# A two-layer language-model tower on one NeuronCore: the tables that give every engine its order are solved anew, with the filler products at other places

## The chip, the cores and the metric

One core of a Trainium2 chip runs the whole program. The metric is the device time of one execution in microseconds (us); the time before is the median of three runs. Five engines work side by side, each through its own list of instructions and in that order alone: TensorE (PE in the profile, with its weight loads as PEld), VectorE (DVE), ScalarE (ACT), GpSimd (POOL) and SyncE (SP), which here only starts DMA transfers. They wait for one another by semaphores.

## The reference

16 sequences of 128 tokens with 256 features go through an embedding with layer norm and four residual blocks. Cut to what matters:

```python
h = tok(x, mask, itok)                       # three table rows added, layer norm
h = h + attn0(layernorm(h))                  # linear attention with random features, relu
h = h + ffn0(layernorm(h))                   # the two nearest of 32 prototypes, rank 16 each
h = h + attn1(layernorm(h))                  # causal softmax attention, 16 heads, rotary
h = h + ffn1(layernorm(h))                   # 256-1024-256 with ternary weights
```

Keys of attn0 share one maximum a sequence, and a sequence needs nothing of another, so each sequence is a tile of its own.

## The kernel before, in words

The kernel works on 16 tiles of 128 tokens by 256 features, kept in one SBUF tensor `hres`. A tile passes through some 130 steps with short names; each name is one branch of the `step` function of its engine. Products that need more than half precision are split into a high and a low half (`xTP`, `wqkT_hi`, `wqkT_lo` and so on), three products for one. The steps that the prediction speaks of are, in the order of one tile:

- embedding: `g` (POOL, two gathers), `e2`, `Est`, `Eag`, `Ers`, `Exn`, `esc`, `eh`
- first attention: `Pst`, `Pag`, `Prs`, `Pxn` (normalised tile `xnP`), `Ptr` or `Phi`, `Plo` and the DMA transposition `PT`, then `qk` and `v` (PE products, L1438), `qhi` and `qlo` (halves of query and key, ACT L1258 and DVE L908), `qT` (DMA transposition, L510), `fQ` and `fK` (features, L1450), `qd` and `kd`, `kmxT`, `kmr`, `kbc` (maximum of the keys, L1605, L937, L1619), `ctx`, `o`, `ont`, `of` (L1637 to L1676)
- prototypes: `Fst` to `Fxn` (`xnF`), `Ftr` (L1706), `prt`, `fh`, `hg`, `hgT` (DMA), `y` (L1778)
- second attention: `Rtr`, `rqk`, `rot`, `rT1` and `rT2` (DMA, `rT<-split`), `s1` (L1898), `ngm`, `rT3` (DMA), `s2` (L1921), `pvx`, `pvT`, `wo`
- last block: `Mtr`, `m1` (L2015), `m2` (L2033), `ob`, and the store `st` (L550).

Steps that are done once prepare weights: `zo1`, `zf1`, `zr3` and others on DVE, `yp1`, `yp2`, `yf1` on ACT, `xo1` (L1469), `xo2` (L1477, L1480) and `xt` (L1487) on PE. `xo1` multiplies the two output matrices of the first attention and waits for the second group of loads (the last is `protoT`). `yp1` makes `wqkT_hi` and `zp1` makes `wqkT_lo`, which `qk` needs.

What sets the order is the table `ORDER`: a string of step names for each engine. `due(engine)` reads it from left to right and gives each name the next tile that has not had it. So the steps of different tiles are interleaved (six or seven tiles are in work at a time), and no engine ever takes a step out of its string's order. A waiting step holds all that stand behind it on its engine.

For the first and the last tiles (`BY_PE`) transpositions are made on PE, for the rest by DMA from SP. All DMAs of SP are started in the order of its string; a transposition that waits for its data holds later ones.

Two tables add products of zeros that nothing reads: `warm_up(94)` runs 94 of them (128x512) at the start (L1461), and `WARM[step][tile]` says how many stand ahead of a step (L1500), after the wait for the PSUM bank and before the wait for the step's data. PE's clock, as the profile shows it, has two levels: 1.2 and 2.4 GHz (a granted clock of 0.50 and 1.00).

## Time and profile before

| what | before |
|---|---|
| median of 3 runs | 462.4 us (460.88 to 462.6) |
| profiled execution, its own time | 467.38 us |
| its span, first to last instruction | 465.6 us |
| PE busy | 395.4 us (85%), 5011 products |
| DVE, ACT, POOL busy | 349.0, 275.8, 293.7 us |
| mean granted clock | 0.956 |

The profiled execution is one run, and 4.98 us above the median. Its span is what the rows below lie in. A busy PE includes the filler products, 94 at the start and 53 later. The profile page also shows that the last 100 us keep DVE, ACT and POOL less busy than the middle, since the tiles run out there.

### The profile page before, as it was taken

The page shows a single profiled execution, that of the slowest core. Times are in us where ns is not written, and L with a number is a line of the kernel's source. Part 1 is how long each engine was busy: PE and PEld are TensorE (multiplying, and loading weights), DVE is VectorE, ACT ScalarE, POOL GpSimd, SP SyncE. Part 2 cuts the span into 40 slices and gives each one's busy share as a digit, 9 for nine tenths or more (in the row PEclk, how much of TensorE's full clock was granted, in tenths as well). Part 3 has the DMA queues.
Part 4 walks back from the last instruction along what each step waited for, and adds up shares of the span by engine and source line. Part 5 has one row for each costly group of instructions (what it writes and reads, how often), then busy time and mean ns, then how long its engine had stood idle before and what let it go on. Part 6 is the DMA issues. An engine that isn't in the chain of part 4 may idle for free.

```text
span 465.6 us, 13969 instructions
## 1 busy us (share of the span) xinstructions
PE 395.4 (85%) x5011; PEld 273.8 (59%) x5011; DVE 349.0 (75%) x937; ACT 275.8 (59%) x605; POOL 293.7 (63%) x431
## 2 busy tenths in 40 slices
...
GB/s 137 175 270 163 181 72 57 69 83 92 85 156 63 129 83 105 136 118 139 115 111 111 117 128 95 109 132 125 86 117 94 101 131 104 72 3 46 14 13 35
DMA packets 145844, 48.56 MB, mean 104 GB/s; under 512 B 137264, under 2 KB 143216, under 8 KB 145776
## 3 DMA queue, kind: packets, MB, share of 16 engines
...
## 4 chain that ended last, share of the span: by engine, by line
PE 33%; POOL 18%; DMA 14%; issue 14%; DVE 9%; ACT 6%; SPq 3%; another core or an unknown queue 1%; POOLq 0%; ACTq 0%; DVEq 0%
PE PS L1438 9%; DMA hgT<-hgs 4%; PE PS L2033 4%; PE PS L1778 3%; DMA qkT<-qs 3%; DMA rT<-split 2%; POOL split L693 2%; PE PS L2015 2%; PE PS L1506 2%; PE PS L1936 2%; DMA xTP<-xsP 2%; POOL wneg L608 2%; POOL stage_f L690 2%; POOL hgs L676 1%; PE PS L1898 1%
## 5 line engine op out<-in xcount | busy, mean ns | idle before, releaser
L1084 DVE TENSOR_REDUCE split<-PS 128x16 f16<-128x2048 f32 x16 | 36.8, 2298 | 6.9 <-PE PS L1506 6.5
L680 POOL TENSOR_TENSOR rstdR<-rstdR,consts 128x1 f32<-128x1 f32 x16 | 8.8, 553 | 37.9 <-DVE rstdR L1043 37.9
L690 POOL TENSOR_TENSOR stage_f<-stage_f 128x512 f32<-128x512 f32 x16 | 20.4, 1272 | 18.7 <-DVE stage_f L1072 8.8
L2015 PE MATMUL PS<-xTM,w1q 128*128 128x128 f16 x512 | 31.4, 219 | 0.0
L2015 PEld LDWEIGHTS PS<-xTM,w1q 128*128 128x128 f16 x512 | 28.6, 98 | 3.6 <-issue 3.6
L1778 PE MATMUL PS<-faT_hi,hgT 128*128 128x256 f16 x128 | 26.7, 295 | 4.0 <-DMA hgT<-hgs 4.0
L1172 ACT ACTIVATE xnR<-hres,nmeanR,rstdR 128x256 f32<-128x256 f32 x16 | 9.6, 599 | 32.1 <-POOL nmeanR L682 32.1
L1438 PE MATMUL PS<-wqkT_hi,xTP 128*128 128x512 f16 x64 | 22.6, 395 | 4.6 <-DMA xTP<-xsP 3.7
L658 POOL TENSOR_TENSOR qe<-qef,qe 128x704 f16<-128x704 f32 x16 | 24.3, 1521 | 1.8 <-issue 1.0
L1637 PEld LDWEIGHTS PS<-va,kp 128*88 128x88 f32 x256 | 21.8, 158 | 2.6 <-issue 0.7
L1461 PE MATMUL PS<-warm 128*128 128x512 f16 x94 | 22.0, 398 | 1.4 <-DVE warm L1139 1.4
L1438 PE MATMUL PS<-rwqk_hi,xTR 128*128 128x512 f16 x64 | 22.6, 394 | 0.4 <-DVE xTR L1051 0.3
L1169 ACT ACTIVATE split<-stage_f 128x256 f16<-128x256 f32 (+1 forms) x48 | 22.0, 481 | 1.4 <-POOL stage_f L690 1.4
L1637 PE MATMUL PS<-va,kp 128*88 128x34 f32 x256 | 22.3, 242 | 0.4 <-issue 0.4
L693 POOL TENSOR_TENSOR split<-stage_f,split 128x512 f16<-128x512 f32 x16 | 18.9, 1182 | 5.3 <-ACT split L1169 5.1
L669 POOL TENSOR_TENSOR dist<-near,halves 128x2 f32<-128x2 f32 x16 | 11.4, 713 | 16.4 <-ACT near L1314 16.3
L1438 PE MATMUL PS<-fbT_hi,xTF 128*128 128x512 f16 x64 | 21.7, 379 | 0.0
L676 POOL TENSOR_TENSOR hgs<-hg,hgs 128x512 f16<-128x512 f32 x16 | 18.5, 1157 | 4.3 <-ACT hgs L1169 4.1
L1450 PE MATMUL PS<-proj_hi,qkT 64*128 64x88 f16 x256 | 14.8, 208 | 6.2 <-DMA qkT<-qs 3.7
...
L700 POOL TENSOR_TENSOR rstdM<-rstdM,consts 128x1 f32<-128x1 f32 x16 | 8.8, 548 | 16.8 <-DVE rstdM L1110 16.8
L1172 ACT ACTIVATE ehat<-esum,nmeanE,rstdE 128x256 f32<-128x256 f32 x16 | 9.5, 592 | 16.7 <-POOL nmeanE L630 16.7
...
## 6 DMA issues: line engine op xcount, KB each, us to landing
...
rT<-split SPq DMA_TRANSPOSE x26, 2.9
```

The source lines that it names most:

```text
L658: g.tensor_tensor(of_pairs(qel), in_pairs(qef), of_pairs(qeh), ALU.subtract).then_inc(qel_ok, 1)
L676: g.tensor_tensor(hgs[:, R2:2 * R2], hg[:, :], hgs[:, 0:R2], ALU.subtract).then_inc(hgl_ok, 1)
L690: g.tensor_tensor(rot[:, :, :].rearrange("p h d -> p (h d)"), rc[:, :], rs[:, :], ALU.add).then_inc(rot_ok, 1)
L693: g.tensor_tensor(slots(32), rot[:, :, :], slots(16), ALU.subtract).then_inc(rl_ok, 1)
L1084: v.tensor_reduce(slots(SLOT - DH)[:, 0:H, DH - 1].rearrange("p (c j) -> p j c", j=4), PS[:, BANK["s1"]:BANK["s1"] + 4, :].rearrange("p j ...
L1169: return a.activation(dst, src, ACT.Copy)
L1172: a.activation(dst, src, ACT.Identity, bias=nmean[x][:, 0:1], scale=rstd[x][:, 1:2]).then_inc(xn_ok[x], 1)
L1438: last = pe.matmul(dst, xT[x][:, xp, :], wp[:, c, :], start=(n == 0), stop=(n == 3 * KC - 1 and bias is None))
L1461: last = pe.matmul(PS[:, SET_BANK, :], warm[:, 0:P], warm[:, :], start=(j == 0), stop=(j == n - 1))
L1637: last = pe.matmul(PS[0:MP, BANK["ctx"], 2 * VA * j:2 * VA * (j + 1)], kp[:, (j % 2 * 4 + j // 2) * MP:(j % 2 * 4 + j // 2 + 1) * MP], va[ ...
L1778: pe.matmul(PS[:, BANK["y"], 0:D], hgT[:, xp, :], wp[:, c, :], start=(c == 0 and xp == 0 and wp is whi["faT"]), stop=False)
L2015: last = pe.matmul(PS[:, BANK["m1"] + f // 4, f % 4 * P:(f % 4 + 1) * P], w1q[:, n % KC, f * P:(f + 1) * P], xT["M"][:, n, :], start=False ...
```

## The change

Every string of `ORDER` is written anew. The steps are the same ones, each as often as before, and every engine still has all of its steps (398 on PE, 737 on DVE, 566 on ACT, 307 on POOL, 152 on SP). 222 of PE's steps stand at another place, by 0.8 places in the mean; 574 of DVE's, by 2.6. The banks of PSUM and the set of transpositions made on PE are untouched. Of the filler products 98 instead of 94 stand at the start, and 39 instead of 53 later, at other steps.

```diff
 ORDER = {
...
     "SP": """
-        lR qT PT lW1 qT qp lW2 PT qp qT PT qp qT hgT PT rT3 qp qT rT2 rT1 hgT onT rT3 PT qp qT rT2 rT1 hgT onT rT3 PT qp qT rT2 rT1 hgT onT rT3 PT qp
...
+        lR qT PT lW1 qT qp lW2 PT qp qT PT qp qT hgT rT3 PT qp qT rT1 rT2 hgT onT rT3 PT qp qT rT2 rT1 hgT onT rT3 PT qp qT rT2 rT1 hgT onT rT3 PT qp
...
     "PE": """
-        xo1 Ptr qk xo2 v fQ qk fK kmxT v kbc fQ ctx fK o ont of kmxT v kbc qk Ftr xt prt ctx fh o hgTp ont fQ y of fK qk kmxT v Rtr kbc Ftr rqk prt
...
+        Ptr qk v xo1 fQ qk fK xo2 kmxT kbc ctx fQ o ont v fK of kmxT kbc qk Ftr prt ctx fh xt v o hgTp ont fQ y of v fK qk kmxT Rtr kbc Ftr rqk prt
...
 WARM = {
-    "qk": {0: 4},
-    "v": {0: 7},
-    "fQ": {0: 9},
-    "kmxT": {0: 4, 2: 2, 3: 4},
-    "ctx": {0: 5, 2: 1},
-    "ont": {0: 2},
-    "Ftr": {0: 2},
+    "qk": {0: 3},
+    "fQ": {0: 8},
+    "ctx": {0: 8, 1: 2, 2: 2},
+    "ont": {0: 3},
+    "Ftr": {0: 4},
     "prt": {0: 3},
-    "rT2p": {0: 2},
-    "y": {1: 3},
+    "rT2p": {0: 1},
...
-            warm_up(94)
+            warm_up(98)
```

**Place 1, the start.** PE from its first instruction, before. `warm` are the fillers, `xnP` the first tile's normalised rows, `wqkT` rows the first `qk`.

```order
L1461 MATMUL PS<-warm 128x512 x94
L1469 MATMUL PS<-wfcT,stage_p 128x256 x4
L1534 MATMUL PS<-ident,xnP 128x128 x2
L1500 MATMUL PS<-warm 128x512 x4
L1438 MATMUL PS<-wqkT_hi,xTP 128x512
L1438 MATMUL PS<-wqkT_lo,xTP 128x512
L1438 MATMUL PS<-wqkT_hi,xTP 128x512 x2
L1438 MATMUL PS<-wqkT_lo,xTP 128x512
L1438 MATMUL PS<-wqkT_hi,xTP 128x512
L1442 MATMUL PS<-rows_all,pick 128x512
```

And now:

```order
L1458 MATMUL PS<-warm 128x512 x98
L1531 MATMUL PS<-ident,xnP 128x128 x2
L1497 MATMUL PS<-warm 128x512 x3
L1435 MATMUL PS<-wqkT_hi,xTP 128x512
L1435 MATMUL PS<-wqkT_lo,xTP 128x512
L1435 MATMUL PS<-wqkT_hi,xTP 128x512 x2
L1435 MATMUL PS<-wqkT_lo,xTP 128x512
L1435 MATMUL PS<-wqkT_hi,xTP 128x512
L1439 MATMUL PS<-rows_all,pick 128x512
```

`xo1` (`wfcT,stage_p`) stood between the fillers and the transposition of `xnP`; now it stands behind `qk` and `v` of tile 0 (not shown), and `v` no longer waits behind `xo2`.

DVE in the same place, before, from the first instruction of `zo1` to `qlo` of tile 0 (`qs<-PS,qs`); `PV` (`xTP`), `Pst` and `Pag` stand ahead of it:

```order
L799 TENSOR_TENSOR proto_sq<-protoT 128x64
L800 TENSOR_SCALAR protoT<-protoT 128x64
L803 TENSOR_TENSOR wneg<-stage_p,bv 128x512
L805 TENSOR_REDUCE bo_v<-wneg 128x2
L807 TENSOR_TENSOR bo_v<-bo_v,bo 128x2
L876 BN_STATS statsE<-esum 128x6
L793 TENSOR_SCALAR proj_hi<-proj 128x176
L795 SCALAR_TENSOR_TENSOR proj_lo<-proj,proj_hi 128x176
L880 BN_AGGR mvE<-statsE 128x2
L882 TENSOR_SCALAR rstdE<-mvE 128x1
L908 SCALAR_TENSOR_TENSOR qs<-PS,qs 128x32x16
```

And now, from `PV` of tile 0 on:

```order
L901 TENSOR_TENSOR xTP<-PS,xTP 128x256
L887 BN_STATS statsP<-hres 128x6
L891 BN_AGGR mvP<-statsP 128x2
L893 TENSOR_SCALAR rstdP<-mvP 128x1
L905 SCALAR_TENSOR_TENSOR qs<-PS,qs 128x32x16
L873 BN_STATS statsE<-esum 128x6
L834 CAST iota_row<-iota_i 1x32
L877 BN_AGGR mvE<-statsE 128x2
L879 TENSOR_SCALAR rstdE<-mvE 128x1
```

`qlo` stood behind the five instructions of `zo1`, behind `Est`, `zp4` (`proj_hi`, `proj_lo`) and `Eag`; now it follows `Pst` and `Pag` directly, and `zo1` comes after it. On ACT `yf1` (`fbT_hi`) moved in the same way from ahead of `qhi` to behind it, and `yp1` (`wqkT_hi`) to behind the second tile's `Exn`.

**Place 2, PE ahead of the prototypes of tile 0.** From `kmxT` of tile 1 on, before:

```order
L1605 MATMUL PS<-ident,kmx 16x128
L1438 MATMUL PS<-wvT_hi,xTP 128x256
L1438 MATMUL PS<-wvT_lo,xTP 128x256
L1438 MATMUL PS<-wvT_hi,xTP 128x256 x2
L1438 MATMUL PS<-wvT_lo,xTP 128x256
L1438 MATMUL PS<-wvT_hi,xTP 128x256
L1619 MATMUL PS<-ident,kmx_row 128x16
L1438 MATMUL PS<-wqkT_hi,xTP 128x512
```

And now, as far as `Ftr` of tile 0 (`ident,xnF`):

```order
L1602 MATMUL PS<-ident,kmx 16x128
L1616 MATMUL PS<-ident,kmx_row 128x16
L1435 MATMUL PS<-wqkT_hi,xTP 128x512
L1435 MATMUL PS<-wqkT_lo,xTP 128x512
L1435 MATMUL PS<-wqkT_hi,xTP 128x512 x2
L1435 MATMUL PS<-wqkT_lo,xTP 128x512
L1435 MATMUL PS<-wqkT_hi,xTP 128x512
L1439 MATMUL PS<-rows_all,pick 128x512
L1497 MATMUL PS<-warm 128x512 x4
L1703 MATMUL PS<-ident,xnF 128x128 x2
```

`v` of tile 2 (the `wvT` rows) stood between `kmxT` and `kbc` of tile 1 and so ahead of `Ftr` of tile 0, with `qk` of tile 2 and two fillers behind it; now it comes after `fh` of tile 0, four fillers stand ahead of `Ftr`, and `kbc` follows `kmxT` with nothing between. In later tiles too (3 to 6, 12 and 13) a `v` left the place between `kmxT` and `kbc`.

**Place 3, the end.** PE from `m1` of tile 14, before:

```order
L2011 MATMUL PS<-sel,b1h 128x512 x2
L2015 MATMUL PS<-xTM,w1q 128x128 x32
L2033 MATMUL PS<-w2q,stage_r 128x256 x16
L1993 MATMUL PS<-ident,xnM 128x128 x2
L1500 MATMUL PS<-warm 128x512
L2011 MATMUL PS<-sel,b1h 128x512 x2
L2015 MATMUL PS<-xTM,w1q 128x128 x32
L2033 MATMUL PS<-w2q,hidden 128x256 x16
L1500 MATMUL PS<-warm 128x512
L2033 MATMUL PS<-w2q,stage_r 128x256 x16
```

And now:

```order
L2008 MATMUL PS<-sel,b1h 128x512 x2
L2012 MATMUL PS<-xTM,w1q 128x128 x32
L2030 MATMUL PS<-w2q,stage_r 128x256 x16
L1990 MATMUL PS<-ident,xnM 128x128 x2
L2030 MATMUL PS<-w2q,hidden 128x256 x16
L1497 MATMUL PS<-warm 128x512
L2008 MATMUL PS<-sel,b1h 128x512 x2
L2012 MATMUL PS<-xTM,w1q 128x128 x32
L1497 MATMUL PS<-warm 128x512
L2030 MATMUL PS<-w2q,stage_r 128x256 x16
```

`m2` of tile 14 stood behind `m1` of tile 15 and now stands ahead of it, right behind the last transposition (`ident,xnM`).

## Rows read from the trace of the kernel before

**Rows 1.** The page: its first line, and the engines' busy time

```profile
span 465.6 us, 13969 instructions
...
PE 395.4 (85%) x5011; PEld 273.8 (59%) x5011; DVE 349.0 (75%) x937; ACT 275.8 (59%) x605; POOL 293.7 (63%) x431
```

**Rows 2.** Busy time by stage; columns: stretch, length, PE, PEld, DVE, ACT, POOL, granted clock, DMA, GB/s

```profile
28.50:69.00 40.50, 28.75 (x229) 15.95 (x230) 31.65 (x80) 24.83 (x46) 32.29 (x44) 0.83 0.62 160
69.00:108.60 39.60, 31.43 (x353) 19.70 (x352) 34.10 (x86) 22.58 (x54) 34.56 (x33) 0.91 0.40 63
108.60:365.50 256.90, 226.62 (x3182) 163.50 (x3179) 209.53 (x564) 172.61 (x388) 173.03 (x262) 0.97 0.65 112
365.50:465.60 100.10, 83.64 (x1151) 63.13 (x1149) 61.86 (x156) 50.78 (x112) 33.66 (x51) 0.98 0.27 56
```

**Rows 3.** Timeline of PE, start: start, duration, instruction, [idle before <- releaser]

```profile
1.42 21.96 PE L1461 MATMUL PS<-warm 128*128 128x512 f16 x94 [1.42 <-DVE warm L1139]
...
25.25 1.97 PE L1469 MATMUL PS<-wfcT,stage_p 128*128 128x256 f32 x8 [1.86 <-DMA protoT<-in_protoT]
27.05 0.38 PE L1534 MATMUL PS<-ident,xnP 128*128 128x128 f32 x2
...
28.52 0.38 PE L1438 MATMUL PS<-wqkT_hi,xTP 128*128 128x512 f16 x1 [0.23 <-DVE xTP L904]
...
37.19 0.21 PE L1450 MATMUL PS<-proj_hi,qkT 64*128 64x88 f16 x2
```

**Rows 4.** Timelines of ACT and DVE, same stretch

```profile
23.37 0.60 ACT L1172 ACTIVATE xnP<-hres,nmeanP,rstdP 128x256 f32<-128x256 f32 x1 [3.96 <-POOL nmeanP L646]
...
29.75 1.06 ACT L1175 ACTIVATE fbT_hi<-stage_f 128x1024 f16<-128x1024 f32 x1 [1.89 <-DMA stage_f<-in_faT]
30.71 0.58 ACT L1258 ACTIVATE qs<-PS 128x512 f16<-128x512 f32 x1
...
32.51 0.68 DVE L908 SCALAR_TENSOR_TENSOR qs<-PS,qs 128x512 f16<-128x512 f32 x1
...
41.51 0.89 DVE L925 TENSOR_TENSOR qd<-PS,qb 128x704 f32<-128x704 f32 x1
```

**Rows 5.** Timeline of SP, which starts the transfers

```profile
22.51 0.43 SPq L457 DMA_DIRECT2D stage_f<-in_faT  x1
...
33.22 1.57 SPq L510 DMA_TRANSPOSE qkT<-qs  x1
```

**Rows 6.** Timelines of PE and ACT around Ftr of tile 0

```profile
59.88 0.37 PE L1438 MATMUL PS<-wvT_hi,xTP 128*128 128x256 f16 x1 [1.48 <-DMA xTP<-xsP]
...
61.24 0.60 PE L1619 MATMUL PS<-ident,kmx_row 16*128 16x16 f32 x2
...
64.74 1.06 PE L1500 MATMUL PS<-warm 128*128 128x512 f16 x2
65.59 0.55 PE L1706 MATMUL PS<-ident,xnF 128*128 128x128 f32 x2
...
61.89 0.60 ACT L1172 ACTIVATE xnF<-hres,nmeanF,rstdF 128x256 f32<-128x256 f32 x1 [1.05 <-POOL nmeanF L664]
```

**Rows 7.** Busy time by stretch: two spells at a granted clock of 0.50

```profile
52.30:65.90 13.60, 9.96 (x53) 4.88 (x50) 10.24 (x25) 8.00 (x12) 12.54 (x17) 0.50 0.55 140
93.20:100.00 6.80, 6.22 (x67) 4.07 (x68) 5.05 (x10) 3.61 (x8) 6.30 (x8) 0.50 0.62 84
```

**Rows 8.** Waits of PE from 108.6 to 365.5: total, times, longest

```profile
PE PS L1898 <- DMA rT<-split: 6.9, 5, 2.3
PE PS L1778 <- DMA hgT<-hgs: 3.2, 3, 1.7
...
PE PS L1619 <- DVE kmx_row L937: 1.7, 4, 0.6
```

**Rows 9.** Timeline of PE, end

```profile
455.90 0.38 PE L1500 MATMUL PS<-warm 128*128 128x512 f16 x1 [1.09 <-DVE xTM L1118]
...
461.06 1.91 PE L2033 MATMUL PS<-w2q,stage_r 128*128 128x256 f16 x16
```

More of the change, by code:

```diff
@@ L75 @@
+        bb e2 Rrs qel esc Frs bb Ers Prs eh dist rot rl Prs hgl gsl Plo rol onl Mrs e2 Rrs qel Frs Mlo esc dist rot Mrs rl gsl Plo hgl Ers onl rol Mlo
+        eh Rrs Frs qel Mrs bb rot dist esc eh rl hgl gsl rol Prs onl Rrs Plo qel Frs bb Mlo bb rot dist rl Mrs rol hgl gsl onl bb Mlo Prs Rrs Plo qel
+        Frs Mrs rot dist rl gsl hgl rol bb qel Rrs Mlo Frs Mrs rot dist rl hgl gsl rol Rrs Mlo Frs Mrs bb dist rot rl gsl hgl Mlo Rrs rot rl bb Mrs
+        Mrs Mrs bb bb bb
     """,
     "DVE": """
-        zi Est Eag zp3 Pst zp1 Est Pag zm Eag PV Pst Pag zo1 Est zp4 Eag qlo zo2 zp2 zf1 zt Pst Est diag Eag qmx Pag qb qd qlo kmx kmr kb kd Est zf2
@@ L78 @@
-        qmx diag qb qd Eag ctl zo3 od on zr3 zf3 oV Pst kmx Pag hP Fst Fag kmr zr1 Est kb kd Eag zr2 FT Pst nd2 top qlo tix gap gt hg ctl zth od Pag
-        on ws hgTb diag oV qmx qb qd hF hP Rst Fst Rag Fag kmx kmr zq1 kb RT kd qlo FT rs2 rs1 nd2 rc top zq2 tix gap ctl gt ws hg od zq3 on rT2b diag
-        rT1b qmx qb oV qd ngm hF Rst Rag hP kmx Fst Fag kmr Pst RT Est kb kd zrm FT Eag rs1 nd2 top rc rs2 tix Pag gap qlo zq4 gt hg ctl ws qmx diag
-        qb od rd on qd ro ngm rV hF Rst Rag kmx hR hP kmr Est Fst Fag RT Mst kb kd rc rs2 Mag rs1 FT nd2 top qlo tix gap gt hg Pst Eag diag rd ctl Pag
```

103 lines of the change are left out of this document (52 added, 51 removed).

## The prediction

> **What bounds the kernel now.** I read the page first, for who is busiest: PE, 395.4 us of a span of 465.6 [rows 1]. Then busy time by stage, since the share of PE is not one thing [rows 2]. From 108.6 to 365.5, while tiles 4 to 14 follow one another, PE is busy 226.62 of 256.9 us; `qk` of tile 4 starts at 108.6 and that of tile 15 at 365.5, so a tile costs 23.4 us, of which 2.8 are idle. That stage and the last 100 us (83.64 of 100.1 busy) go by PE's work, and the work is the same after the change. From 28.5 to 108.6 it is another matter: PE is busy 60.2 of 80.1 us, with the fillers in it, DVE 65.8 and POOL 66.9. There the first tiles' chains set the pace, from engine to engine, and PE waits. A microsecond saved on the first tile's chain moves all that follows, as long as POOL and DVE, with 13 to 14 idle microseconds each in this stage, can follow.
>
> Third the timelines of the start, for what holds that chain. PE runs its 94 fillers from 1.42 to 23.4, then waits 1.86 for the load of `protoT`, does `xo1` (1.97 us) and only at 27.05 transposes `xnP`, which was there from 23.97 on (23.37 + 0.60); `qk` of tile 0 starts at 28.52 [rows 3, 4]. ACT copies its high half at 30.71, behind `fbT_hi` and a load; DVE makes the low half at 32.51, behind `zo1`; SP starts the transposition `qT` at 33.22, and `fQ` of tile 0 runs at 37.19 [rows 3 to 5].
>
> **The change, part by part.**
>
> 1. *`xo1` behind `qk` and `v`, four more fillers.* The fillers cost 21.96 / 94 = 0.23 us each in that row, so 98 end at 24.3. On ACT the second tile's `Exn` and `yp1` (1.06, as `fbT_hi`, which has its shape) now stand ahead of `xnP`. If they fit into ACT's idle 3.96 us ahead of it, `Ptr` starts at 24.3; if both fall wholly behind, at 23.97 + 0.60 + 1.06 = 25.6. I take 24.5, nearer to the first, since that idle time is longer than both. Gain 27.05 - 24.5 = 2.55 us, between 1.4 and 2.75. What is late next is `zp1`, which waits for `yp1`; `Ptr`'s copies hide most of it.
> 2. *`qlo` ahead of `zo1`, `qhi` ahead of `yf1`.* From the start of `qk` to that of `qlo` it takes 3.99 us now. Without the work ahead it is 1.7 for `qk`, 0.58 for `qhi` and 0.1 of hand-over, 2.4. Gain 1.6. `qT` then starts at 33.22 - 2.55 - 1.6 = 29.1.
> 3. *But `qT` then meets the loads.* At 33.22 nothing is left of them and `fQ` follows 3.97 us after the start of the transfer. At 29.1 the weights of the second attention are still on their way. What a transfer takes in that crowd, the load of `faT` shows: started at 22.51, released ACT at 29.75, 7.2 us. So `fQ` of tile 0 comes between 29.1 + 4.0 = 33.1 and 29.1 + 7.2 = 36.3. A transposition is smaller than that load, but behind it; I take 34.4, a little below the middle. Gain at `fQ`: 37.19 - 34.4 = 2.8, between 0.9 and 4.1.
> 4. *From there to `of` of tile 0.* The same steps in another order. `qd` (41.51) was followed by `kmx` and `kd`; now `Pst`, `qlo` of tile 1, `zr3` and `zo2` come between, and `yo` stands ahead of `ke` on ACT. Against that, `v` of tile 0 and `fQ` no longer stand behind `xo2`, and `zo3` is done ahead of `ctl`. I take the two as equal: nothing, and the 2.8 go on.
> 5. *Ahead of `Ftr` of tile 0.* `xnF` was there at 62.49, `Ftr` ran at 65.59: PE was behind, with `v` of tile 2 (59.88 to 61.24), `kbc`, `qk` and two fillers [rows 6], all at a granted clock of 0.50 [rows 7]. `v` goes, 1.36 us; two more fillers come, 0.43 each at this level and 0.21 at the upper. Gain 0.5 to 0.9; I take 0.7.
> 6. *`kbc` right behind `kmxT`.* Of tiles 3 to 6, 12 and 13 `v` no longer covers `kmr`, so PE waits there about what it waits at the worst now, 0.6 us [rows 8], instead of 0.3: 6 x 0.3 = 1.8 at most. The same `v` now covers other waits of PE (it stands mostly ahead of `kmxT`). Nothing net, the bounds are 0 and 1.8 slower.
> 7. *Fillers.* 10 fewer. They stood where PE waits, so their 2.1 us give nothing back. What they cover if gone is the clock, a rival below.
> 8. *The middle.* All other moves, 574 of DVE's steps among them, shift waits. PE waits there for transfers: 6.9 us in 5 waits for `rT`, 3.2 in 3 for `hgT` [rows 8]. No row tells which end. I take nothing, with one half of these two gone (5.0 faster) and as much again (5.0 slower) as bounds.
> 9. *The end.* `m2` of tile 14 (1.91, as the last one) goes into the idle 1.09 us plus filler ahead of `m1` of tile 15 [rows 9]: `m1` starts 0.5 later and all behind it too. Cost 0.5.
>
> Sum: -2.8 - 0.7 + 0.5 = **-3.0 us**. Against the profiled execution that is 467.38 - 3.0 = 464.4. It stands 4.98 above the median of the runs, 462.4; the same gain from the median gives **459.4 us**.
>
> The Trainium skill speaks against part 3 being free: DMA: Bandwidth & Descriptors, section Issuing engines are not separate DMA queues, says that all transfers run on the same 16 DMA engines and interleave. By that rule the transposition shares with the loads, and the sum would be that of the far end of part 3, with 2.8 - 0.9 = 1.9 us less gained, 461.3.
>
> **Rivals.** *The start's gain is lost on the way* (0.27). The far ends of parts 1 to 3 together, or POOL: it has 66.9 us of work in 80.1, and its long single steps stand in it unmoved, so tiles 1 to 3 may reach 108.6 hardly earlier. For it speaks that tile 1 waits for POOL's chain; against it, 13 us of idle time. Then the time is 461 to 463.
>
> *The middle gets shorter too* (0.16). Half the waits of part 8 go: -3.0 - 5.0 gives 454.4. For it speaks that order is all that these waits depend on; against it, that the rows do not show one that must end.
>
> *The clock* (0.12), slower. Now the lower level of 1.2 GHz holds from 52.3 to 65.9 and from 93.2 to 100.0, in a stage in which PE is idle a quarter of the time [rows 2, 7]. 11 of the fillers that stood ahead of `v` and `kmxT` of tile 0 are gone, and of the 10 of tiles 1 to 3 six. A spell like that at 93.2, with PE busy 6.22 of 6.80 us, holds some 3.1 us that the upper level would have saved. Two more of them in this stage cost 6.2: 459.4 + 6.2 = 465.6. One costs less than the change gains, so two is the point from which it decides. The Trainium skill says of this, in TensorE: Matmul & The Clock Gate, section HAM oscillation, that idle gaps between bursts of products bring the clock down; by that rule fewer fillers in the waiting stage cost time, and the trace agrees in so far as both spells follow waits.
>
> *The middle waits longer* (0.11), slower. Steps that give late transfers room stand further from what they feed; six more waits like those for `rT`, 1.4 us each, and the 0 to 1.8 of part 6 make 459.4 + 8.3 = 467.7; three of them already eat the gain. For it speaks part 6, where products that covered a wait have left it; against it, that PE has 2.8 idle microseconds a tile to take small shifts.
>
> That the change doesn't do what it says is no case of its own: the order of the instructions shows it done.
>
> **How the numbers follow.** The forecast, a gain kept from 2.3 to 5 us, has 0.34. About 0.5% (2.3 us) is what a measurement of this kernel can tell from no change. Faster by more: forecast and shorter middle, 0.34 + 0.16 = 0.50. Within: the lost gain, 0.27. Slower: 0.12 + 0.11 = 0.23. The range takes in the shorter middle nearly whole and the clock's rival, and leaves out the worst of the longer middle: 453.5 to 466.5.
>
> **What would show it.** `Ptr` of tile 0 at 24 to 25.6, `qT` at 29 to 30, `fQ` of tile 0 at 33 to 36.3; `Ftr` of tile 0 at 61 to 63; `qk` of tile 4 at 104 to 106.5; after that still 23.4 us a tile. The clock's rival would show as more than 20.4 us at 0.50 before 108.6. Wrong would be: `qk` of tile 4 at 108 or later (the gain lost), or a tile in the middle that costs less than 23.1 or more than 23.7 us, since ten of them then outweigh the start.

## The result, and the profile after

The changed kernel takes **471.26 us** (470.42 to 472.38, 4 runs) where the kernel before took 462.5 in the same comparison (460.88 to 464.49, 4 runs): a ratio of 1.0154, 95% interval 1.0113 to 1.0195. It is slower; 459.4 us was forecast, in a range that ended at 466.5.

How large the loss is, four runs did not settle. Repeated on three chips beside the kernel before, the same program stood nearer to it. In these tables the medians are over all executions, which spread over some 15 us of either kernel; the ratios and their intervals leave the slower ones out, so for a spread like this I go by the medians.

| the changed kernel | executions | median us | kernel before, same chip | difference | ratio, interval |
|---|---|---|---|---|---|
| first measurement | 4 | 471.26 | 462.5 (4) | +8.8 | 1.0154 [1.0113, 1.0195] |
| `after_again`, chip 4 | 12 | 461.59 | 459.85 (17) | +1.7 | 0.9969 [0.9916, 1.0022] |
| `after_third`, chip 1 | 12 | 466.69 | 464.64 (23) | +2.1 | 0.9993 [0.9941, 1.0044] |
| `after_fourth`, chip 8 | 6 | 469.89 | 464.21 (17) | +5.7 | 1.012 [1.005, 1.019] |

All four differences of the medians point the same way; by the ratios the first and the last measurement are slower and the two between are level with the kernel before. The three repeats, by the means of all executions weighted with their own scatter, give +2.7 us with a 95% margin of 1.5; the first gives +8.7 with 1.7. I take some 3 us, 0.6%, as what the change costs by itself, and come back at the end to what lies above.

**The page of the changed kernel**, against [rows 1]:

```profile
span 470.1 us, 13951 instructions
...
PE 394.0 (84%) x5001; PEld 274.6 (58%) x5001; DVE 348.2 (74%) x937; ACT 274.8 (58%) x605; POOL 293.2 (62%) x431
```

4.5 us more span, with 1.4 us less PE work, and the other engines within 1 us. Nothing was added; the time is in waits.

**Busy time by stage**, cut at the start of `qk` of tile 4 (107.3) and of tile 15 (369.4), against [rows 2]; columns: stretch, length, PE, PEld, DVE, ACT, POOL, granted clock, DMA share, GB/s:

```profile
28.50:69.00 40.50, 27.42 (x227) 16.40 (x225) 30.89 (x79) 25.39 (x51) 30.73 (x43) 0.87 0.64 170
69.00:107.30 38.30, 29.38 (x328) 19.14 (x329) 31.68 (x81) 20.30 (x46) 33.72 (x34) 0.87 0.31 56
107.30:369.40 262.10, 227.07 (x3184) 164.15 (x3185) 210.00 (x567) 173.05 (x393) 173.68 (x264) 0.96 0.63 111
369.40:470.10 100.70, 83.47 (x1151) 62.95 (x1149) 61.99 (x154) 50.15 (x110) 32.90 (x49) 0.98 0.24 53
```

Up to `qk` of tile 4 the change is ahead: 107.3 against 108.6. From there to tile 15 it takes 262.1 us against 256.9, with PE busy 227.07 against 226.62: all but 0.5 of the 5.2 us is idle time of PE, 35.0 us instead of 30.3. The rest is as long as before to within a microsecond.

**The start on PE**, against [rows 3]; columns: start, duration, instruction, [idle before <- releaser]. The line numbers of the changed kernel are lower by 3:

```profile
1.42 23.61 PE L1458 MATMUL PS<-warm 128*128 128x512 f16 x98 [1.42 <-DVE warm L1136]
24.87 0.38 PE L1531 MATMUL PS<-ident,xnP 128*128 128x128 f32 x2
...
26.35 0.38 PE L1435 MATMUL PS<-wqkT_hi,xTP 128*128 128x512 f16 x1 [0.45 <-DVE xTP L901]
...
27.86 0.27 PE L1435 MATMUL PS<-wvT_hi,xTP 128*128 128x256 f16 x1
...
30.24 1.89 PE L1497 MATMUL PS<-warm 128*128 128x512 f16 x8
35.52 0.22 PE L1447 MATMUL PS<-proj_hi,qkT 64*128 64x88 f16 x2 [3.39 <-DMA qkT<-qs]
```

And **ACT, DVE and SP** in the same stretch, against [rows 4, 5]:

```profile
28.06 0.60 ACT L1255 ACTIVATE qs<-PS 128x512 f16<-128x512 f32 x1 [2.38 <-issue]
...
28.69 0.69 DVE L905 SCALAR_TENSOR_TENSOR qs<-PS,qs 128x512 f16<-128x512 f32 x1 [1.75 <-ACT qs L1255]
...
29.40 1.50 SPq L507 DMA_TRANSPOSE qkT<-qs  x1
```

`Ptr` comes 2.2 us earlier, `qlo` 3.8 earlier, SP starts `qT` at 29.40 instead of 33.22. But `fQ` gains only 1.7 us: eight fillers run, and then it still waits 3.39 us for `qkT`, which lands 6.1 us after its start. In the kernel before that transfer landed 3.2 us after its start; `fQ` ran 0.8 us later, right behind nine fillers and not on the landing. The DMA moved 319 GB/s in the 6.1 us from 29.4, and 75 GB/s in the 4.0 us from 33.2 before.

**Ahead of `Ftr` of tile 0** on PE, against [rows 6]:

```profile
60.49 1.03 PE L1497 MATMUL PS<-warm 128*128 128x512 f16 x4
61.35 0.38 PE L1703 MATMUL PS<-ident,xnF 128*128 128x128 f32 x2
```

`Ftr` runs at 61.35, 4.2 us earlier than before.

**Waits of PE in the middle**, 107.3 to 369.4, against [rows 8]; columns: waiting line <- releaser: total us, times, longest:

```profile
PE PS L1918 <- DMA rTm<-split: 6.6, 6, 2.2
PE PS L1895 <- DMA rT<-split: 5.7, 5, 1.7
PE PS L1435 <- DVE hres L1030: 4.4, 4, 1.6
PE PS L1616 <- DVE kmx_row L934: 3.6, 8, 0.5
PE PS L1775 <- DMA hgT<-hgs: 2.5, 2, 2.2
```

The kernel before, from 108.6 to 365.5, in two rows of the same view:

```profile
PE PS L1921 <- DMA rTm<-split: 1.2, 1, 1.2
...
PE PS L1438 <- DVE hres L1033: 0.4, 2, 0.2
```

Two rows are the new ones. L1918 is `s2`, the second pass over the scores of the second attention. It reads `rTm`, which `rT3` transposes once `ngm` has put the negated maxima of `s1` into `split`: 6.6 us, where the same row of the kernel before had 1.2. L1435 <- `hres` L1030 is `wo`, which writes into PSUM bank 7 and so waits until DVE's `hF` has read `y` out of it: 4.4 us, 0.4 before. The row of `kmx_row` doubled, 3.6 in 8 waits for 1.7 in 4; those for `rT` and `hgT` fell by 1.2 and 0.7. The three rows that grew hold 11.3 us more together and PE's idle time only 4.7, so most of what they hold was waited for elsewhere before: a row's growth is not its price.

**The end on PE**, against [rows 9]: the last two `m2` steps. The last one starts 3.4 us later, in a span that is 4.5 us longer.

```profile
458.01 1.92 PE L2030 MATMUL PS<-w2q,hidden 128*128 128x256 f16 x16
...
464.46 1.91 PE L2030 MATMUL PS<-w2q,stage_r 128*128 128x256 f16 x16 [1.89 <-DVE stage_r L1120]
```

### The profile page after: what moved, and what is told of

Same layout as the page of the kernel before. It is cut to its first block, busy times and chain, and to the rows that moved or that the text cites. A ratio compares the mean times of both kernels' runs of the same rounds, so it can differ in the third digit from the quotient of the medians.

```text
span 470.1 us, 13951 instructions
## 1 busy us (share of the span) xinstructions
PE 394.0 (84%) x5001; PEld 274.6 (58%) x5001; DVE 348.2 (74%) x937; ACT 274.8 (58%) x605; POOL 293.2 (62%) x431
## 4 chain that ended last, share of the span: by engine, by line
PE 47%; DVE 16%; DMA 13%; issue 9%; ACT 7%; POOL 4%; SPq 2%; another core or an unknown queue 2%; ACTq 0%; DVEq 0%; POOLq 0%
PE PS L1435 13%; DMA rTm<-split 6%; PE PS L1458 5%; PE PS L2012 4%; DVE split L1081 4%; PE PS L2030 3%; PE PS L1933 3%; PE PS L1634 2%; DMA rT<-split 2%; DMA hgT<-hgs 2%; DMA qkT<-qs 2%; PE PS L1447 2%; PE PS L1918 2%; PE PS L1503 2%
## 5 line engine op out<-in xcount | busy, mean ns | idle before, releaser
L1081 DVE TENSOR_REDUCE split<-PS 128x16 f16<-128x2048 f32 x16 | 36.8, 2297 | 13.7 <-remote 8.2
L1435 PE MATMUL PS<-rwqk_hi,xTR 128*128 128x512 f16 x64 | 25.8, 447 | 0.7 <-DVE xTR L1048 0.3
L1458 PE MATMUL PS<-warm 128*128 128x512 f16 x98 | 23.6, 407 | 1.4 <-DVE warm L1136 1.4
L1435 PE MATMUL PS<-wqkT_hi,xTP 128*128 128x512 f16 x64 | 22.0, 385 | 1.4 <-ACT stage_p L1386 0.8
L1435 PE MATMUL PS<-fbT_hi,xTF 128*128 128x512 f16 x64 | 21.7, 380 | 0.0
L1380 ACT ACTIVATE stage_p<-PS 128x1024 f32<-128x1024 f32 x16 | 16.4, 1023 | 6.6 <-PE PS L1503 6.5
L1447 PEld LDWEIGHTS PS<-proj_hi,qkT 64*128 64x128 f16 x256 | 10.4, 100 | 15.8 <-issue 8.2
```

The lines of the kernel that those rows point to most:

```text
L1081: v.tensor_reduce(slots(SLOT - DH)[:, 0:H, DH - 1].rearrange("p (c j) -> p j c", j=4), PS[:, BANK["s1"]:BANK["s1"] + 4, :].rearrange("p j ...
L1435: last = pe.matmul(dst, xT[x][:, xp, :], wp[:, c, :], start=(n == 0), stop=(n == 3 * KC - 1 and bias is None))
L1447: last = pe.matmul(PS[:, bank + i, MP * c:MP * (c + 1)], qkT[rows_, c0 + c, :], part[rows_, MP * i:MP * (i + 1)], start=(c == 0 and part i ...
L1458: last = pe.matmul(PS[:, SET_BANK, :], warm[:, 0:P], warm[:, :], start=(j == 0), stop=(j == n - 1))
```

## The experiments

Sixteen kernels ran, four to a chip, each with the kernel before beside it. Theory M says that the loss lies in the new order of the middle; theory H that the new head brings it on, whatever comes behind; a third, that the placing of the fillers and with it the clock does. A kernel with two orders in one follows, on every engine, the one up to the instant at which PE starts the named step, and the other behind it; each step still runs once.

| run | chip | executions | median us | before | difference | ratio, interval |
|---|---|---|---|---|---|---|
| `head_new` | 7 | 12 | 458.43 | 459.08 | -0.6 | 0.9978 [0.9938, 1.0018] |
| `head_new2` | 1 | 12 | 464.25 | 464.64 | -0.4 | 0.9953 [0.9908, 0.9997] |
| `head_old` | 7 | 12 | 465.61 | 459.08 | +6.5 | 0.9984 [0.9905, 1.0063] |
| `head_old2` | 8 | 12 | 469.43 | 464.21 | +5.2 | 1.0088 [1.0045, 1.0132] |
| `fill_old` | 7 | 6 | 466.47 | 459.08 | +7.4 | 1.0177 [1.0123, 1.0231] |
| `fill_new` | 1 | 6 | 470.88 | 464.64 | +6.2 | 1.0111 [1.0051, 1.017] |
| `wo_back` | 7 | 12 | 460.87 | 459.08 | +1.8 | 0.9984 [0.987, 1.0099] |
| `wo_back2` | 1 | 6 | 473.24 | 464.64 | +8.6 | 1.0144 [1.0078, 1.021] |
| `wo_ahead` | 4 | 6 | 468.16 | 459.85 | +8.3 | 1.024 [1.0169, 1.0311] |
| `s2_back` | 4 | 7 | 475.14 | 459.85 | +15.3 | 1.0362 [1.0305, 1.0418] |
| `pe_mid_new` | 4 | 6 | 533.75 | 459.85 | +73.9 | 1.1683 [1.1608, 1.1759] |
| `cut8_new` | 8 | 6 | 470.55 | 464.21 | +6.3 | 1.0125 [1.0054, 1.0197] |
| `cut8_old` | 8 | 6 | 473.66 | 464.21 | +9.5 | 1.0233 [1.0159, 1.0306] |

**Head and middle apart.** `head_new` is the changed kernel with the old orders behind `qk` of tile 4. PE's string around the seam:

```diff
-        ctx fh o rT2p rT1p fQ ont s1 of y rv fK s2 Rtr kmxT kbc rqk Ftr qk prt ctx pvx fh pvT o v fQ s1 rv rot_ y of fK wo s2 Rtr kmxT kbc rqk Ftr qk
+        ctx fh o rT2p rT1p fQ ont s1 of y rv fK s2 Rtr kmxT kbc rqk Ftr prt qk fh pvx ctx v pvT fQ o s1 rot_ rv y fK wo of kmxT Rtr s2 kbc rqk Ftr qk
```

> The new orders of all five engines and the new zero products up to qk of tile 4, the old orders behind it. Theory M (the new order of the middle, qk of tile 4 to qk of tile 15, costs the 262.1 us against 256.9 that the two profiles show): the middle falls back to 256 to 258.5 us, qk of tile 4 starts at 106.5 to 108, and the time is that of the kernel before less the 1.3 us of the head, 459.5 to 463. Theory H (what the new head leaves behind, later buffers and other low-clock stretches, slows the tiles after it, whatever their order): the middle stays at 261 to 263 us and the time at 468 to 472.

> The changed head with the old orders from qk of tile 4 on, again. Theory M: 0.1 to 0.5% faster than the kernel before, as the first time (458.4 beside 459.1), and faster than the changed kernel by its whole loss plus the head's gain. If the head's gain does not reach the end: equal to the kernel before within 0.3%.

`head_old` is the mirror image, made in the same way.

> The mirror image: the old orders and zero products up to qk of tile 4, the new orders behind it. Theory M: the middle stays at 261 to 263 us, and the time is 469 to 473. Theory H: the middle is 256 to 258.5 us and the time 461 to 465.

> The old orders and zero products up to qk of tile 4, the new ones behind, a second time. Theory M: slower than the changed kernel by the 1.5 to 4 us of its missing head, and than the kernel before by 1.0 to 1.5%, as the first time (465.6 beside 459.1). If the middle's 259 us against 252 in the profiles so far were chance: within 0.4% of the kernel before.

The middle of `head_new`, from its `qk` of tile 4 to that of tile 15, by busy time and by waits of PE:

```profile
107.80:354.20 246.40, 220.88 (x3183) 160.46 (x3180) 208.55 (x563) 172.20 (x387) 171.92 (x260) 0.99 0.63 115
```

```profile
PE PS L1895 <- DMA rT<-split: 3.6, 5, 1.7
PE PS L1435 <- DMA xTo<-xso: 3.4, 6, 1.0
...
PE PS L1616 <- DVE kmx_row L934: 1.7, 4, 0.6
...
PE PS L1435 <- DVE hres L1030: 0.4, 2, 0.2
```

And `head_old2`, the head and the middle:

```profile
0.00:111.10 111.10, 91.32 (x687) 50.77 (x688) 77.76 (x221) 53.68 (x108) 86.56 (x120) 0.85 0.52 131
111.10:368.80 257.70, 223.11 (x3181) 162.07 (x3178) 209.17 (x564) 171.79 (x389) 173.21 (x262) 0.98 0.61 110
```

And PE's waits in that middle of `head_old2`:

```profile
PE PS L1921 <- DMA rTm<-split: 6.8, 5, 1.9
...
PE PS L1619 <- DVE kmx_row L937: 4.5, 9, 1.0
...
PE PS L1438 <- DVE hres L1033: 3.4, 4, 1.1
```

With the old order the middle is 246.4 us (250.5 the second time), the row of `rTm` is gone from the list and `wo <- hF` is back at 0.4. With the new one behind the old head it is 257.7 (259.7 the first time), the three rows are there, and `head_old` and `head_old2` are 6.5 and 5.2 us slower than the kernel before in their medians, 5.7 us by the means of both (margin 2.0). By its ratio alone, 0.9984 with only two executions in it, `head_old` is not slower; `head_old2` is, 1.0088. That is theory M; H is out, since the new head did not bring the loss with it. A limit stays: a seam may cost something by itself, as those at tile 8 below suggest, and no run prices that for tile 4. `head_new` has a seam too and loses nothing.

Parts of M's forecast failed. `head_old2` should have been 1.5 to 4 us slower than the changed kernel, whose head it lacks, and stands 0.5 us below it on the same chip. Both `head_new` should have kept the head's gain, and are only 0.6 and 0.4 us faster than the kernel before. Their `qk` of tile 4 starts at 107.8 and 111.2, no earlier in the mean than in the kernels with the old head. One thing in it is the cut itself: in the old string, and so in `head_new` too, `prt` stands ahead of that `qk`, in the changed kernel behind it (the diff shows it); with its wait it took 0.6 us in the kernel before and 1.2 in the first `head_new`. Of the kernels that ran, `head_new` is the only one whose median was not above that of the kernel before. By the means of both runs it is 0.9 us faster with a margin of 1.5, a gain that these runs can't tell from zero.

All profiles together, microseconds from `qk` of tile 4 to that of tile 15, each with PE's idle time in it:

| | profiles | length | mean | PE idle, mean | PE busy, mean |
|---|---|---|---|---|---|
| old middle (before, `head_new`, `head_new2`, `fill_new`) | 4 | 256.9, 246.4, 250.5, 255.2 | 252.3 | 28.5 | 223.8 |
| new middle (the changed kernel) | 4 | 262.1, 255.9, 258.4, 261.3 | 259.4 | 33.3 | 226.2 |
| new middle behind the old head | 2 | 259.7, 257.7 | 258.7 | 33.1 | 225.6 |
| new middle, old fillers (`fill_old`) | 1 | 259.2 | 259.2 | 30.9 | 228.3 |

The new middle of the changed kernel costs 7.1 us by the first two rows, 4.8 of it idle time and 2.4 the same products at a lower granted clock. Four profiles a side that scatter so leave a margin of some 7 us, and the two of `head_new` weigh heavily: their middles had 2.8 and 3.4 us at the low level of the clock, the other two old ones 17.1 and 13.7, the seven new ones 10.8 to 24.6. Without `head_new` the difference is 3.3 us. What does not depend on the draw of the profiles is the pattern of waits: `rTm` holds 5.2 to 8.1 us, `kmx_row` 3.6 to 4.5 and `wo <- hF` 1.8 to 4.7 in all seven new middles, and at most 1.2, 1.8 and 0.4 in the four old ones.

The executions tell more than the profiles. At equal time at the low level (worked out for each execution as in the last section, with one slope for each pair of kernels), the changed kernel stands 2.2, 2.1 and 2.9 us above the kernel before in its three repeats (margins 1.5 to 1.7), the two `head_old` 3.3 and 3.9 (1.2 and 1.4), the two `head_new` 2.0 and 0.0 (1.2 and 1.4). So the three repeats agree once the clock is taken out, and of the 5.7 us of `head_old` some 3.6 are there at an equal clock; the rest goes with 6.7 and 2.8 us more low time. `head_new` had 6.3 and 4.4 us less of it than the kernel before. Whether an order brings such low time or only drew it, these runs do not separate.

**The changed kernel three times more.** No edit.

> The changed kernel unaltered, to have it on the same chip as the other runs. The runs so far on this chip put the kernel before at 459.1 us, with executions from 451.6 to 465.2 whose time follows the granted clock, and the changed head or the changed zero products with the new middle at 465.6 and 466.5. Theory M expects 464 to 468 us here, a middle of 259 to 262 us, and the row L1918 <- rTm at 4 us or more; if the first measurement was a draw of low clock alone, it comes at 458 to 461.

> The changed kernel unaltered once more, beside the four others of this batch. Its first four executions were at 470.4 to 472.4 us, twelve on another chip at 454.1 to 469.8 with a median of 461.6 beside 459.9 for the kernel before. If the true difference is the small one and the first measurement a draw: a ratio of 1.000 to 1.008. If the large one is true and the second a draw: 1.012 to 1.019.

> The changed kernel unaltered, beside the three others. On two chips its median stood 1.7 and 2.1 us above that of the kernel before (12 and 12 executions), on the first 8.8 us (4 executions). If 2 us is the true difference: a ratio of 1.000 to 1.009 here too; if the difference swings by chip, 1.012 or more is possible again.

The small difference came out twice, and one in between, so neither expectation held for all three. Theory M had expected a middle of 259 to 262 us in `after_again`; it was 255.9, with the row of `rTm` at 7.2. `after_fourth`, head and middle:

```profile
0.00:105.70 105.70, 84.33 (x668) 47.61 (x669) 76.35 (x218) 52.25 (x104) 88.13 (x120) 0.90 0.55 135
105.70:367.00 261.30, 229.54 (x3186) 165.33 (x3185) 210.06 (x567) 173.10 (x392) 172.62 (x262) 0.95 0.61 111
```

Head 105.7, middle 261.3, as in the first profile. In all four profiles the row of `rTm` is 5.2 to 7.2 us, that of `kmx_row` 3.6 in 8 waits, that of `wo <- hF` 2.0 to 4.7: the waits belong to the order and not to one execution.

**The fillers alone.** `fill_old` is the changed kernel with the old table and start, `fill_new` the kernel before with the new ones; of the latter:

```diff
-    "qk": {0: 4},
-    "v": {0: 7},
-    "fQ": {0: 9},
-    "kmxT": {0: 4, 2: 2, 3: 4},
+    "qk": {0: 3},
+    "fQ": {0: 8},
...
-            warm_up(94)
+            warm_up(98)
```

> The changed kernel with the zero products of the kernel before (94 at the start and 53 later against 98 and 39), all orders as changed. If where the zero products stand moves the stretches of low granted clock and these set the time (0.50 for 46.2 us in all against 43.4 before): the sum of low stretches falls to about 43, the time by 1 to 3 us to 468 to 470. Theories M and H both: within 1 us of the changed kernel, 470 to 472, whatever the stretches do.

> The kernel before with the changed kernel's zero products (98 at the start and 39 later against 94 and 53), orders as before. If they cost by themselves, as fewer products while TensorE waits in tiles 0 and 1 leave longer stretches at a granted clock of 0.50: 462 to 465 us, qk of tile 4 at 109 to 112. If not, within 0.3% of the kernel before.

`fill_new`, busy time up to its `qk` of tile 4, of a stretch in it, and of the middle:

```profile
0.00:112.40 112.40, 89.19 (x677) 50.73 (x678) 77.75 (x219) 52.30 (x107) 86.55 (x118) 0.83 0.52 126
45.00:63.00 18.00, 13.76 (x104) 8.58 (x103) 13.82 (x32) 12.24 (x22) 14.18 (x20) 0.53 0.64 154
112.40:367.60 255.20, 226.13 (x3182) 163.26 (x3179) 208.94 (x565) 172.42 (x387) 172.73 (x262) 0.97 0.64 113
```

The same orders as in [rows 2], and `qk` of tile 4 comes at 112.4 instead of 108.6. The granted clock of the head is 0.83 where it was 0.91: a stretch of 18 us at 0.53 stands where 13.6 us at 0.50 stood [rows 7], and in single microseconds the low level adds up to 37.4 us before tile 4, against 20.4 before. The middle is untouched, 255.2. `qk` came about where the first theory expected it (109 to 112), and the time rose by more than it expected. `fill_old` shows the same in its one profile from the other side: `qk` of tile 4 at 112.4, clock 0.86 up to there. The two such pairs stand 6.2 and 7.4 us above the kernel before. For the new fillers with the old orders the cost is shown; for the old fillers with the new orders it is not told apart from the changed kernel's own spread. The expectation that theories M and H gave for `fill_old`, the time of the changed kernel (470 to 472), was put in absolute microseconds and tells little on a chip where the kernel before is at 459.1. Beside it, +7.4 us stands against the +1.7 to +8.8 of the changed kernel elsewhere; on this chip the changed kernel did not run.

**`wo` moved back, and moved ahead.** `wo_back` is the changed kernel with `wo` behind `of` and `fK` in eight tiles:

```diff
-        kbc rqk Ftr pvx prt qk Mtr ctx pvT fh m1 fQ o v m2 s1 y rv of fK wo Rtr s2 kmxT rqk kbc Mtr Ftr qk prt pvx fh ctx pvT m1 o v fQ s1 m2 y rv wo
-        of fK s2 Rtr kmxT kbc rqk pvx Ftr qk prt pvT ctx fh m1 fQ o v m2 s1 rv y fK wo of Rtr s2 kmxT rqk kbc pvx Ftr qk prt pvT m1 fh v ctx fQ m2 o
+        kbc rqk Ftr pvx prt qk Mtr ctx pvT fh m1 fQ o v m2 s1 y rv of fK wo Rtr s2 kmxT rqk kbc Mtr Ftr qk prt pvx fh ctx pvT m1 o v fQ s1 m2 y rv of
+        fK wo s2 Rtr kmxT kbc rqk pvx Ftr qk prt pvT ctx fh m1 fQ o v m2 s1 rv y fK of wo Rtr s2 kmxT rqk kbc pvx Ftr qk prt pvT m1 fh v ctx fQ m2 o
```

> The changed kernel with wo moved back behind of and fK on TensorE in eight tiles of the middle, all else as changed. If wo right behind y in one PSUM bank is what costs in the middle (the wait for VectorE's hF took 4.4 us there against 0.4 before): that row falls to 1 us or less, the middle gets 3 to 4 us shorter, and the time is 467 to 468.5. If the wait only moves (TensorE waits next for kmx_row, rT or rTm, because those chains set the time of a tile): the row falls as well, but the middle stays within 1 us of 262.1 and the time at 470 to 472.

> The changed kernel with wo moved back behind of and fK in eight tiles, beside the changed kernel itself this time. If wo behind y costs in the changed order: 3 us or more faster than it. If the wait only moves: within 1.5 us of it.

Waits of PE in the middle of `wo_back2`:

```profile
PE PS L1895 <- DMA rT<-split: 4.9, 5, 1.7
PE PS L1813 <- ACT xnR L1169: 4.8, 3, 1.8
...
PE PS L1435 <- DMA xTo<-xso: 2.6, 2, 1.6
...
PE PS L1435 <- DVE hres L1030: 1.1, 2, 1.0
```

The row `wo <- hF` fell to 1.1 us, and `rTm` to 2.8 (L1918). But `xnR` rose to 4.8 and `xTo` came with 2.6, the middle is 257.8 us (258.4 in the changed kernel on that chip), in an execution of 466.31 that was the shortest of this kernel. Beside the changed kernel on the same chip (466.69) the median is 6.6 us higher, where 3 us lower was the forecast of the theory. The first run, whose 460.87 had looked like a gain against 471.26, had no changed kernel on its chip and stood 1.8 us above the kernel before. The wait moved, and that `wo` behind `y` is the cause by itself is out. If the wait only moved, the time should have stayed within 1.5 us; what the rest of the 6.6 is, stays open, and the six executions leave a margin of 5 us. `wo_ahead` asks the same of the kernel before, with `y`, `rv`, `wo`, `of` and `fK` in the new order among themselves in nine tiles:

```diff
-        rqk kbc pvx Ftr Mtr qk prt pvT fh ctx m1 fQ v o m2 s1 rv y fK wo of kmxT Rtr s2 kbc rqk Ftr pvx qk prt Mtr pvT fh ctx m1 v o fQ s1 m2 y of rv
-        wo fK s2 Rtr kmxT kbc rqk pvx Ftr qk prt pvT fh ctx m1 fQ o v m2 s1 rv y of fK wo kmxT Rtr s2 kbc rqk Ftr qk prt pvx fh ctx m1 pvT v o fQ s1
+        rqk kbc pvx Ftr Mtr qk prt pvT fh ctx m1 fQ v o m2 s1 y rv of fK wo kmxT Rtr s2 kbc rqk Ftr pvx qk prt Mtr pvT fh ctx m1 v o fQ s1 m2 y rv wo
+        of fK s2 Rtr kmxT kbc rqk pvx Ftr qk prt pvT fh ctx m1 fQ o v m2 s1 rv y fK wo of kmxT Rtr s2 kbc rqk Ftr qk prt pvx fh ctx m1 pvT v o fQ s1
```

> The kernel before with only y, rv, wo, of and fK put in the changed kernel's order among themselves in nine tiles (2 to 10). If that piece costs what its undoing gave (466 to 460.9, some 5 us): 462 to 465 us, with a row wo <- hF (L1438 <- hres L1033) of 3 us or more. If wo behind y costs only in company of the changed kernel's other orders: 457.5 to 461 us.

```profile
PE PS L1898 <- DMA rT<-split: 8.3, 7, 2.2
PE PS L1605 <- DVE kmx L933: 3.7, 4, 2.3
...
PE PS L1438 <- DVE qd L925: 3.0, 3, 1.3
```

8.3 us slower, more than expected, and not by the row that was expected: `wo <- hF` is not in the list at all. PE waits instead for `kmx` (3.7) and `qd` (3.0), steps that DVE still does in the places of its old order.

**`s2` put back.** The changed kernel with `s2` behind `Rtr` (and `kmxT` where it was so) again in eight of the tiles 1 to 10, and with `kbc` and `rqk` as before there:

```diff
-        prt pvx ctx fh v pvT fQ o s1 rv rot_ y fK of wo s2 Rtr kmxT kbc rqk Mtr Ftr qk prt pvx fh pvT ctx m1 fQ o v s1 rv rot_ y fK wo of s2 Rtr kmxT
+        prt pvx ctx fh v pvT fQ o s1 rv rot_ y fK of wo Rtr s2 kmxT rqk kbc Mtr Ftr qk prt pvx fh pvT ctx m1 fQ o v s1 rv rot_ y fK wo of Rtr s2 kmxT
```

> The changed kernel with s2 put back behind Rtr and kmxT, as before, in eight tiles (1 to 10), with kbc and rqk as before too; wo stays where the change put it. If s2 too early (waiting for rTm, 6.6 us in the middle against 1.2) is a cause beside wo: the row L1918 <- rTm falls to 2 us or less and the time to 461 to 464. If s2's wait only fills time in which the chain through s1, the softmax and pvx would have waited anyway: the row falls, the time stays at 465 to 468, and a later row (rT, kmx_row) takes it up.

```profile
PE PS L1918 <- DMA rTm<-split: 4.5, 4, 2.0
PE PS L1602 <- DVE hres L1098: 3.3, 2, 2.0
PE PS L1435 <- DVE xTR L1048: 3.2, 4, 0.8
```

15.3 us slower than the kernel before. The row of `rTm` only fell from 7.2 (`after_again`, same chip) to 4.5, and PE now waits for `hR` (L1098, 3.3) and for DVE's copy of `xTR` (3.2), which it had not waited for. Neither theory for this run allowed for a loss, and it is 13.6 us against the changed kernel on the same chip.

**PE's new order alone.** The kernel before with only PE's string changed from `qk` of tile 4 on:

```diff
-        ctx fh o rT2p rT1p fQ ont s1 y rv of fK kmxT Rtr s2 kbc Ftr rqk prt qk fh pvx ctx v pvT fQ o s1 rot_ rv y fK wo of kmxT Rtr s2 kbc rqk Ftr qk
+        ctx fh o rT2p rT1p fQ ont s1 y rv of fK kmxT Rtr s2 kbc Ftr rqk prt qk ctx pvx fh pvT o v fQ s1 rv rot_ y of fK wo s2 Rtr kmxT kbc rqk Ftr qk
```

> The kernel before with TensorE's order alone changed to the new one from qk of tile 4 on; VectorE, ScalarE, GpSimd and SyncE keep their old orders. Theory M-PE (the loss lies in TensorE's new order): 463 to 468 us, rows of wo <- hF and s2 <- rTm together 4 us or more in the middle. Theory M-other (it lies in the orders of the others, VectorE's above all): within 2 us of the kernel before, 457 to 461. A mix of one engine's new order with the old ones of the rest fits worse than either whole, so a time above 468 tells nothing between the two.

```profile
PE PS L1657 <- DVE ctl L949: 10.1, 7, 2.4
PE PS L1438 <- DVE qd L925: 9.9, 5, 3.2
PE PS L1619 <- DVE kmx_row L937: 6.4, 8, 1.5
```

533.75 us. PE waits 10.1 us for `ctl` and 9.9 for `qd`, each a step of DVE that stands later in the old string than the new order of PE wants it. The strings of two engines from two solutions do not fit: this run says nothing on which engine holds the loss, as its expectation allowed, but it prices the misfit.

**A seam at tile 8.** Made as `head_new` and `head_old` are, with the exchange at `qk` of tile 8 instead of tile 4; of `cut8_new`, PE's string at the exchange:

```diff
-        kbc rqk Ftr pvx prt qk Mtr ctx pvT fh m1 fQ o v m2 s1 y rv of fK wo Rtr s2 kmxT rqk kbc Mtr Ftr qk prt pvx fh ctx pvT m1 o v fQ s1 m2 y rv wo
+        kbc rqk Ftr pvx prt qk Mtr ctx pvT fh m1 fQ o v m2 s1 y rv of fK wo Rtr s2 kmxT rqk kbc Mtr Ftr pvx qk prt pvT fh ctx m1 v o fQ s1 m2 y of rv
```

> The new orders up to qk of tile 8, the old ones behind. Profiles so far: tiles 4 to 7 take 93.7 us in the mean of five with the new orders, 90.6 in the mean of four with the old; tiles 8 to 11 95.6 against 93.1. If the loss is spread over the middle: tiles 4 to 7 at 92.5 to 96, tiles 8 to 11 at 91 to 94, and the time 1 to 2 us below the changed kernel. If it sits in the tiles up to 8 alone: the time of the changed kernel; if behind 8: that of the kernel before less its head's gain, 0.3 to 0.6% faster.

> The old orders and zero products up to qk of tile 8, the new ones behind. Loss spread over the middle: tiles 4 to 7 at 89 to 91.5, tiles 8 to 11 at 93.5 to 97, and 1 to 3 us above the kernel before. Loss in the tiles up to 8 alone: within 0.3% of the kernel before. Loss behind 8: 4 us or more above it.

Measured for tiles 4 to 7 and 8 to 11, from the starts of `qk`: `cut8_new` 96.8 and 94.6 us, `cut8_old` 92.0 and 101.6. Tiles 4 to 7 follow their order, 96.8 with the new and 92.0 with the old one, though both took more than their ranges; over all profiles but that of `pe_mid_new` they take 90.6 to 96.9 us with new orders and 89.1 to 92.0 with old ones. But the two times, +6.3 and +9.5 us, sum to far more than the changed kernel's +5.7 on the same chip, so the parts do not add up; the 101.6 behind the seam is more than in any kernel without one there (89.7 to 99.1, but for `pe_mid_new`). None of the three cases that were laid out fits both runs. Where in the middle the loss lies is inconclusive but for tiles 4 to 7 holding some of it.

## Why the prediction was wrong

By its own parts, with the four profiles of the changed kernel for each.

Parts 1 to 3, the start: right. `Ptr` at 24.8 to 25.4 (24.5 forecast), `qT` at 29.4 to 30.0 (29.1), `fQ` of tile 0 at 34.6 to 35.5 (34.4, between 33.1 and 36.3). The lower bound was read wrongly: the 4.0 us from the start of `qT` to `fQ` were not the transfer, which had landed after 3.2, but the nine fillers ahead of `fQ`. The transposition that now meets the loads took 6.1, 5.5, 4.6 and 5.7 us to its landing in the four profiles. That transfers share the DMA engines, which the Trainium skill says (DMA: Bandwidth & Descriptors, Issuing engines are not separate DMA queues), fits these rows; the far end of part 3 gave 1.9 us less gain than the sum, and the first profile shows 1.1 less.

Parts 4 and 5: `Ftr` of tile 0 at 60.1 to 61.4, forecast 61 to 63. Right, a little better.

`qk` of tile 4 at 103.6 to 107.3, mean 105.7; forecast 104 to 106.5. How much of that is the head's gain, forecast as 3.5 us, is less sure. The old strings stand unchanged up to there in six profiles: 108.6, 108.9, 111.1, 105.8 (`cut8_old`), 109.2 (`wo_ahead`) and 106.2 (`pe_mid_new`), mean 108.3. The new ones do in eight, the four of the changed kernel and those of `wo_back`, `wo_back2`, `s2_back` and `cut8_new`: 102.5 to 107.4, mean 105.9. The gain is 2.4 us by these, with a margin of 2.3, and 0.6 of it is `prt`, which now stands behind that `qk`. The rival that the gain is lost on the way is neither shown nor out: at the end of the program `head_new` keeps 0.9 us of it, margin 1.5.

Part 6, `kbc` right behind `kmxT`, taken at 0 with 1.8 us as the slower bound: the row of `kmx_row` is 1.9 us longer (3.6 for 1.7), the bound itself. Whether the steps that moved away saved as much in other rows, no run separates. They are not all `v`, as this part and the text on place 2 have it: `v` stood between `kmxT` and `kbc` in tiles 0 to 2 only. In tiles 5, 6, 12 and 13 it was `rqk` that left the place, in tiles 3 and 4 `Rtr` and `s2`.

Part 7, the fillers, taken at nothing: wrong as a statement about them. The new set on the old order costs 6.2 us, so what is right is only that in company of the new order the low-clock stretches of the head came out about as long as before (20.4 us in both first profiles, 13.6 to 23.7 in the four of the changed kernel). The price I gave the clock's rival was too high: 17.0 us more at the low level in `fill_new` are 2.5 spells like that at 93.2, 7.8 us at 3.1 each, and 3.8 us were lost at tile 4 and 6.2 at the end. Its rule, fewer fillers in the waiting stage cost time, held for `fill_new`. It did not hold with the order that the fillers were placed for, so fillers and order had to be taken together.

**Part 8, the middle, is the step that failed**: "I take nothing", with 5.0 us either way as bounds. Measured: 5.2 us longer in the first profile against the one that I read, 7.1 by the means of four profiles each (margin 7), and 5.7 us of time (margin 2.0) when the new orders stand behind the old head. The argument that the kernel has 2.8 us of idle time a tile in which small shifts are absorbed was wrong: in 11 tiles the idle time itself rose, from 30.3 to 35.0 us in the first profiles and from 28.5 to 33.3 in the means. The sign that was named for it, a tile of more than 23.7 us, came in two of the four profiles of the changed kernel (23.8, 23.3, 23.5, 23.8). I had looked at the largest rows of the old profile, `rT` and `hgT`, and asked how much of them could go or double. They changed least. The new waits came at `s2`, whose row had 1.2 us before, and at `wo`, which had 0.4. That is the rival "the middle waits longer", 467.7 us and a chance of 0.11, and it was right in kind and of the size (8.3 us); it names two of the three rows, `kmx_row` by part 6 and, as a late transfer, `rTm`. That these rows are what costs the time is not shown: neither attempt to take one away made the changed kernel faster than it was on the same chip.

Part 9, the end, at 0.5 us of cost: from `qk` of tile 15 to PE's last product 95.6 to 98.4 us, 97.4 before. Nothing to be seen of it.

So -0.9 for the new head and +5.7 for what lies behind it, each by its own kernels, give +4.8 us with a margin of 2.5; the three repeats measured +2.7 (margin 1.5) and the first +8.7 (1.7). The sum fits between them and settles neither. The profile that I read was a long execution (467.38 for a median of 462.4), and its 23.4 us a tile were 22.9 in the mean of the four old middles; no term of the sum hangs on that, since the gain was taken from the median.

Left open: why the first four executions stood 8.7 us apart. Their profile shows the same head, middle and rows as `after_fourth`; no run here tells what that chip, or those executions, added. Open too is which engine's order causes the middle's waits: PE's string, the only one that was exchanged alone, met the misfit first. Whether the new orders would do better where transfers land later was not tried.
